# Windowed attention on one core: both heads' score products of a key tile first, then both band masks

## The reference, cut to what matters

```python
attn = jnp.einsum('bqhmd,bkhd->bhmqk', q, k) * sm_scale
q_pos = jnp.arange(L)[:, None]
k_pos = jnp.arange(L)[None, :]
mask = (q_pos >= k_pos) & (q_pos < k_pos + SW)          # SW = 64: these pairs are removed
attn = jnp.where(mask, -jnp.inf, attn)
sink = jnp.broadcast_to(s[:, :, :, None, None], attn.shape[:-1] + (1,))
w = jax.nn.softmax(jnp.concatenate([attn, sink], axis=-1), axis=-1)[..., :-1]
out = jnp.einsum('bhmqk,bkhd->bqhmd', w, v).reshape(B, L, NQ * HD)
```

## Time and profile before

| | |
|---|---|
| time, median of 3 runs | 2771.74 us (2770.3 to 2782.01) |
| the profiled execution | 2764.51 us, its span 2762.8 us |
| TensorE busy over the span | 2515.4 us, 91% |
| VectorE, ScalarE, GpSimd busy | 59%, 46%, 47% |
| score products of the windowed attention | 634 to 1331 us of the span |
| mean granted TensorE clock | 0.936 of full speed |

### The profile page before, as it was taken

The page is one execution under the profiler, slowest core; times in us unless marked ns, Lnnn a source line. Parts: engine busy times, 40 slices in busy tenths (PEclk is TensorE's granted clock), DMA queues, the critical chain, the costliest instruction groups (busy, mean ns, idle before and its releaser), DMA issues. The chain is left out here.

```text
span 2762.8 us, 40694 instructions
## 1 busy us (share of the span) xinstructions
PE 2515.4 (91%) x14474; PEld 1675.7 (61%) x14474; DVE 1625.1 (59%) x2163; ACT 1259.8 (46%) x2174; POOL 1290.9 (47%) x1130
## 2 busy tenths in 40 slices
PE   6887999888999999999878878889999988998798
PEld 4443777654444444444564436678888877776676
DVE  4663555576766766665336543477777745555655
ACT  4464333464555555555434652256655643333322
POOL 4100344486888888888630002255454533442243
PEclk9798999998999999999976989899999999999899
DMA  1000111121101111010000001100010001110111
GB/s 59 1 2 11 39 46 46 48 80 39 39 16 39 31 31 39 16 35 1 25 26 1 1 1 49 47 20 28 20 32 20 20 5 42 46 46 21 31 41 43
DMA packets 39710, 81.63 MB, mean 30 GB/s; under 512 B 7553, under 2 KB 21121, under 8 KB 39041
## 3 DMA queue, kind: packets, MB, share of 16 engines
q1 hardware_dynamic: 39264, 79.41, 10.2%
q10 hardware_dynamic: 288, 0.13, 0.0%
HBM read 59.07 MB, written 2.62 MB: 22 GB/s over the span
## 5 line engine op out<-in xcount | busy, mean ns | idle before, releaser
L2019 DVE TENSOR_REDUCE a1h_mseg<-bank 128x2 f32<-128x1024 f32 x256 | 302.6, 1221 | 187.2 <-PE bank L1776 173.2
L63 POOL TENSOR_TENSOR f_wh<-f_raw,ones_r 128x768 fp32r<-128x768 f32 (+1 forms) x74 | 112.5, 1520 | 534.9 <-PE bank L462 360.0
L1953 ACT ACTIVATE a1h_prob<-bank 128x512 f32<-128x512 f32 x366 | 206.1, 598 | 165.6 <-PE bank L1836 83.8
L1756 POOL TENSOR_TENSOR a_qk<-a_qk,a1h_prob 128x512 f32<-128x512 f32 x186 | 238.9, 1318 | 50.8 <-ACT a1h_prob L1953 50.8
L451 PE MATMUL bank<-x_norm_h,f_wh 128*128 128x512 f32 x592 | 243.1, 411 | 6.7 <-PEq L3249 2.5
L451 PE MATMUL bank<-x_norm_l,f_wh 128*128 128x512 f32 x592 | 237.5, 401 | 0.0
L451 PE MATMUL bank<-x_norm_h,f_wl 128*128 128x512 f32 x592 | 237.0, 400 | 0.0
L658 DVE SCALAR_TENSOR_TENSOR f_tf<-bank,f_bias,f_sg 128x512 f32<-128x512 f32 x148 | 110.9, 750 | 187.2 <-PE bank L451 180.8
L542 ACT ACTIVATE f_hhi<-f_hf 128x512 fp32r<-128x512 f32 x124 | 78.3, 632 | 275.6 <-DVE f_hf L666 275.6
L1834 PE MATMUL bank<-a1h_ql,a1h_k 128*128 128x512 f32 x512 | 203.2, 397 | 0.0
L1849 PE MATMUL bank<-a1h_prob,a_v 128*64 128x512 f32 x732 | 179.9, 604 | 0.0
(11 more groups left out here) (597 smaller groups left out, 6277.1 us busy)
## 6 DMA issues: line engine op xcount, KB each, us to landing
f_raw<-in_l_w_dram SPq DMA_DIRECT2D x66, 385.0 KB, 3.0
a1h_st_q<-a_qk SPq DMA_DIRECT2D x128, 128.0 KB, 2.4
l2a_qkraw<-in_l2a_wqk_dram SPq DMA_DIRECT2D x32, 128.0 KB, 2.1
l2a_vraw<-in_l2a_wvg_dram SPq DMA_DIRECT2D x8, 512.0 KB, 3.7
f_raw<-in_l_w_dram SPq DMA_DIRECT2D x8, 449.0 KB, 3.3
a_qk<-l_keys SPq DMA_DIRECT2D x24, 128.0 KB, 2.7
a1p_raw<-in_l1a_w_dram SPq DMA_DIRECT2D x20, 128.0 KB, 2.1
a_qk<-in_l1a_wo_dram SPq DMA_DIRECT2D x16, 128.0 KB, 2.1
```

Of the source, the lines that this page charges most:

```text
L63: return pool.tensor_tensor(dst, src, one.to_broadcast(list(src.shape)), ALU.mult)
L1756: pool.tensor_tensor(out, first, slot_of[t % NP], ALU.add).then_inc(sum_done, 1)
L1953: act.activation(slot_of[t % NP], core.bank[2 + t % 3][:, :], ACT.Exp, scale=scale).then_inc(p_ready, 1)
L2019: dve.tensor_reduce(mseg[:, :, qb, s], spare(("A", n, k))[:, :, :], AX.X, ALU.max).then_inc(a_read, 1)
```

## The change

The function `scores` now issues a key tile of both heads at once. Its waits and its two products run for head 0 and then for head 1; only after these come the two band masks, head 0 and head 1. Before, each head's mask stood right behind its own two products. A tile without a mask raises s_ready at its second product, as before. The number of instructions, their operands, the banks and the counts of the semaphores are the same.

```diff
--- before.py
+++ after.py
@@ -1810,32 +1810,36 @@
                                    tile_position=(0, 64 - 64 * a))
                 mm.then_inc(a_ready, 1)
 
-            def scores(n, i, a):
+            def scores(n, i):
+
                 h, kb = TILES[i]
                 G = n // 4
-                t = tile(n, i, a)
-                bank = core.bank[2 + t % 3]
-                if i == 0:
-                    pe.wait_ge(m_rows, rows_of(n) + a + 1)
-                    pe.wait_ge(q_lo, PER * n + a + 1)
-                if n == 0 and i == TB:
-                    pe.wait_ge(m_rows, rows_of(n, "N") + a + 1)
-                if i == 0 and a == 0:
-                    if n == 0:
-                        pe.wait_ge(k1_ones, PER)
-                    if n % 4 == 0:
-                        pe.wait_ge(k1_act, G + 1)
-                        pe.wait_ge(k1_dve, G + 1)
-                if t >= 3:
-                    pe.wait_ge(p_ready, t - 2)
                 keys = slice(kb * P, (kb + 1) * P)
                 lo, hi = max(kb * P, h * HALF), min(kb * P + BAND, (h + 1) * HALF)
-                pe.matmul(bank[:, :], kn[:, G % 2, a, keys], QA[n % 2][:, a, half(h)], start=True, stop=False)
-                mm = pe.matmul(bank[:, :], k1[:, a, keys], ql[:, n % 2, a, half(h)], start=False, stop=lo >= hi)
-                if lo < hi:
-                    mm = pe.matmul(bank[:, lo - h * HALF:hi - h * HALF], core.ident_b[:, :],
-                                   mk[:, 0, lo - kb * P:hi - kb * P], start=False, stop=True)
-                mm.then_inc(s_ready, 1)
+                for a in range(PER):
+                    t = tile(n, i, a)
+                    bank = core.bank[2 + t % 3]
+                    if i == 0:
+                        pe.wait_ge(m_rows, rows_of(n) + a + 1)
+                        pe.wait_ge(q_lo, PER * n + a + 1)
+                    if n == 0 and i == TB:
+                        pe.wait_ge(m_rows, rows_of(n, "N") + a + 1)
+                    if i == 0 and a == 0:
+                        if n == 0:
+                            pe.wait_ge(k1_ones, PER)
+                        if n % 4 == 0:
+                            pe.wait_ge(k1_act, G + 1)
+                            pe.wait_ge(k1_dve, G + 1)
+                    if t >= 3:
+                        pe.wait_ge(p_ready, t - 2)
+                    pe.matmul(bank[:, :], kn[:, G % 2, a, keys], QA[n % 2][:, a, half(h)], start=True, stop=False)
+                    mm = pe.matmul(bank[:, :], k1[:, a, keys], ql[:, n % 2, a, half(h)], start=False, stop=lo >= hi)
+                    if lo >= hi:
+                        mm.then_inc(s_ready, 1)
+                for a in range(PER if lo < hi else 0):
+                    bank = core.bank[2 + tile(n, i, a) % 3]
+                    pe.matmul(bank[:, lo - h * HALF:hi - h * HALF], core.ident_b[:, :],
+                              mk[:, 0, lo - kb * P:hi - kb * P], start=False, stop=True).then_inc(s_ready, 1)
 
             def values(n, j):
 
@@ -1898,8 +1902,7 @@
                         values(n - 1, 7)
                     if n < BATCHES:
                         for i in (2 * j, 2 * j + 1):
-                            scores(n, i, 0)
-                            scores(n, i, 1)
+                            scores(n, i)
                         if n == 0 and j < 2:
                             for ks in LATE[j]:
                                 visit(0, ks)
```

## The result

The kernel with the change took 2797.80 us (median of 6 runs, 2786.19 to 2802.88), the kernel before, in the runs beside it, 2771.02 us (6 runs, 2761.31 to 2782.01). The ratio is 1.0078, with a 95% interval of 1.0055 to 1.0101: about 22 us slower, between 15 and 28 (the medians alone lie 26.8 apart). The forecast was 2795 us. The profiled execution of the changed kernel took 2798.34 us.

What follows compares the result with a forecast made beforehand. TensorE, busy 587.80 of 600 us, was taken to set the pace; step losses summed to +22.7, say 23 us, on 2771.7, giving 2795 us, with 2780 to 2806 for 8 in 10.

Steps and rivals of the forecast that it cites:

- step 7: Last step of a batch, ending with a 128-column mask: 2.85 us against 2.51, +0.34 in 16 batches, 5.4 in all.
- The margin of 0.16 us: In old banded steps, the second key tile's head-1 load came 0.16 us later than the first tile's head-0 exponential allowed.
- The place of B1's load: Weight load of the second key tile, head 1, in a fully banded step: 2.05 us after the first load, formerly 1.76.
- The second mask: Grouped masks on TensorE: the second adds 0.09, 0.07 or 0.04 us by width, bounds 0.03 and 0.13.
- Rival 1: The exponential's wait does not bind, leaving only the regrouping gain: about -7 us, 2765 us; chance 0.06.
- Step 0: First step of a batch: +0.50 us in nine batches, +0.36 in three, zero in the others; 5.6 in all.
- Step 5: Step with one banded tile: load stays, the second tile's head-0 mask comes behind; +0.04 us per batch, 0.6 in all.
- three steps 0: First steps of the fourth, eighth and twelfth batches: VectorE's split of keys hides the 0.50 us, so zero.
- signs named: Expected in the profile: ScalarE waits about 110, 0.8 us and more before the load, TensorE about 95% busy, clock 1.00.
- Rival 2: TensorE's waits behind banded steps give the loss back, at most 14 us in the stage: +9, 2781 us; chance 0.07.
- Rival 3: TensorE's stalls lower its clock; a tenth of the stage running slow gives 2855 us; chance 0.03.
- Rival 4: Waits chain through late slots or queries, 0.3 us more in each of 64 steps: +42, 2814 us; chance 0.04.

Runs made afterwards that it cites:

- e4_late1: Kernel before the change, with one tiny ScalarE copy ahead of the first key tile's head-0 exponential in three steps per batch; score stage 697.3 us against 696.5.
- e4_late3: Kernel before the change, with three chained tiny ScalarE copies ahead of the first key tile's head-0 exponential in three steps per batch; stage 716.6 us against 696.5.
- e2_second_pair: Changed kernel with masks grouped only for each step's second key tile; 2770.41 us, ratio 0.9996 to the kernel before; stage 693.5 us.
- e6_filled6: Changed kernel with half of the preceding step's value products put between the two key tiles, in one step per batch; stage 715.4 us against 718.4.
- e3_filled: Changed kernel with half of the preceding step's value products put between the two key tiles, in three steps per batch; stage 737.2 us against 718.4.

## Why the prediction was right

The forecast was that the kernel slows down, through one wait, by 23 us; the stage grew by 21.9. Step by step, over 16 batches:

| step | forecast, us | measured, us |
|---|---|---|
| 0 | 5.6 | 7.3 |
| 1 | 5.3 | 5.1 |
| 2, 3, 4 | 0 | 0.0 |
| 5 | 0.6 | 0.1 |
| 6 | 5.8 | 5.9 |
| 7 | 5.4 | 3.3 |

(By periods; the last batch's step 7 has no successor, so it is left out of the 3.3. It is another 0.35.)

- The margin of 0.16 us. Right: an end 0.146 later is free, and one 0.61 later moves B1's load by 0.45 (e4_late1, e4_late3).
- The place of B1's load: 2.05 forecast, 2.06 in the step shown and 2.07 as a median; the step 2.90, against 2.91 and 2.92.
- The second mask 0.09, 0.07 and 0.04 behind the first for 192, 128 and 64 columns, estimated from narrow masks: 0.093, 0.066 and 0.039 between the starts in the trace. Rival 1's side of it, a small gain by regrouping, exists as well, and e2_second_pair shows it without the wait.
- Step 0: 0.50 on average in the nine batches where A1 waits for VectorE's row, and 0.40 in the three where it doesn't, against 0.50 and 0.36.
- Step 5: 0.04 forecast per batch, 0.01 measured. The sign is right; why the narrow pair is cheaper still was not settled by a run.
- Two terms were off, and by chance against each other. I had put three steps 0 at zero, since the next work there waits for VectorE's split of keys. They grew by 0.57 us each, 1.7 us in all. The hiding was right: in e6_filled6, whose step 0 has the order of the change, one of these three had the short copy, 0.70 us instead of 1.25, and that step grew by 0.01; the two with the long copy grew by 0.57 and 0.58. What failed was that I had taken the split itself as fixed: its copy became 0.57 us longer. And of the three steps 7 that come before new keys, two became 0.69 us shorter instead of 0.34 longer and one 0.46 longer, 2.0 us less than in the sum. The copies are the subject of the last section. That the sum of 22.7 came within 1 us of 21.9 owes something to this luck.
- The first batch, put at zero, became 0.25 us shorter in its steps 0 and 1.
- Of the signs named, three were off in size. The waits on ScalarE rose to 131, not to about 110: those of step 5 and three at a step's start were not counted. Between B0's second product and B1's load lie 0.58 us, not 0.8 and more; that figure does not come out of the prediction's own times either, which have B1's load 0.58 behind where it would otherwise be. TensorE's busy share fell to 96%, for 95%.
- Rival 2 (given back by other waits) fell: steps 2, 3 and 4 did not change, and apart from the copies and the first batch no step got shorter. Rival 3 (the clock): 1.00 in 700 to 1300, before and after. The Trainium skill ("TensorE: Matmul & The Clock Gate", on PSUM-queue depth-cycling) tells of a kernel whose clock swings with short idle times between banks. Here 64 waits were added, each 0.63 us without a load and about 0.2 without a product, and the clock did not swing. Rival 4 (chained waits) did not come either: ScalarE was late by a step's end and on time at the next one's start.

What the copies cost or gave was not tried by itself: it is read from the traces only. That B1's wait could be removed by a fourth bank was not tried, since all eight banks are in use.

## What to carry to other kernels

When instructions of two chains are regrouped to save a little on the busiest engine, look at which result of the group is asked for first: a buffer that comes round after three tiles turns a later first result into a wait of the producer itself. Measure the margin of that hand-over in the trace (here 0.16 us: the load came 0.21 after the end of the exponential instead of the usual 0.05) before spending it; in this kernel the same grouping lost 17 us where the tile was the next to be asked for, and gained 3 where it was not. Work that stands between two steps may be the cover of another engine's work, so moving it into one gap can open a larger one.

## What the runs showed of the hardware

VectorE's copies of keys have no fixed duration. The two copies, each first before and then after the change, and the first of them once more in e6_filled6 (duration in ns: shortest, median, longest; first and last start):

```profile
L2007 DVE CAST a1h_kn<-a_qk x6: 675/676/676, 730.9 to 1123.5; 128x1024 fp32r<-128x1024 f32 x6
```

```profile
L2010 DVE CAST a1h_kn<-a_qk x6: 1245/1248/1255, 737.6 to 1142.2; 128x1024 fp32r<-128x1024 f32 x6
```

```profile
L2013 DVE CAST a1h_kn<-a_qk x6: 702/1245/1251, 735.4 to 1139.7; 128x1024 fp32r<-128x1024 f32 x6
```

```profile
L2014 DVE CAST a1h_k<-a1h_kn x3: 1721/1722/1722, 818.1 to 1167.4; 64x1024 fp32r<-64x1024 f32 x3
```

```profile
L2017 DVE CAST a1h_k<-a1h_kn x3: 690/691/1825, 827.9 to 1187.7; 64x1024 fp32r<-64x1024 f32 x3
```

The first went from 676 to 1248 ns in all six batches, the second from 1722 to 691 in two of three, with the same operands. In the traces it goes by what GpSimd is doing. In all 81 copies of the nine traces of this case, one of two things is seen. Either the copy takes 0.68 to 0.72 us, and the sum that GpSimd has beside it takes 1.7 to 1.8 us instead of 1.28. Or the copy ends 0.54 to 0.56 us behind the end of a sum in flight, however long that is: 1.11 us where the sum ended 0.57 us after the copy's start, 1.25 where it ended 0.70 after it, 1.69 where it ended 1.14 after it, 1.72 to 1.83 where it ended 1.17 to 1.27 after it. The Trainium skill ("SBUF — State Buffer", the section on SBUF's two separate sides) says that VectorE, in a mode that uses two ports, and GpSimd take a shared pair of ports as an exclusive lock: the one that starts first has it for the whole instruction, and the other one stands. The times agree with that; which mode the copies run in no trace here shows. Moving TensorE's work by a third of a microsecond changed which of the two came first, and with it 1.0 us at the end of a batch and 0.57 at the start of another. VectorE's small operations on the row maxima in the first batch, 0.17 us with GpSimd idle and 1.1 to 1.2 us beside its sums (e3_filled, e4_late1), are the same kind of case: a wait of 2.4 to 4.3 us on TensorE hung on them.

ScalarE's exponentials also came closer together: two take 1.09 us where the masks of both heads come together (952.66), and 1.18 where each waits for its own mask (938.01 in the kernel with the second pair grouped). It gave nothing back, since TensorE waits for the first of the two.
